# Cross-attention and mixture of experts: the order of the head on four engines is changed

## The reference

```python
q = layernorm(x) @ Wq.T ; k = v = ctx @ Wq.T
x = x + softmax(causal(q @ k.T / sqrt(128))) @ v
f = layernorm(x)
logits = f @ gate_W                       # 8 experts, the two largest are kept
cw = weights of the two largest, normalised, zero elsewhere
x = x + f + sum over e of cw[:, e] * (relu(f @ W1[e] + b1[e]) @ W2[e] + b2[e])
```

## Time and profile before

| | before |
|---|---|
| median of 3 runs | 132.61 us (131.99 to 133.05) |
| the profiled execution | 132.61 us, its span 130.8 us |
| TensorE busy (matmul) | 122.1 us, 93% |
| TensorE weight load busy | 92.1 us, 70% |
| VectorE busy | 106.1 us, 81% |
| ScalarE busy | 93.2 us, 71% |
| GpSimd busy | 53.1 us, 41% |
| TensorE's granted clock | full in all 40 slices |

### The profile page before, as it was taken

One profiled execution on the slowest core, in us unless ns is written; L12 is line 12 of the kernel. 1 busy time (PEld: TensorE's weight loads), 2 busy tenths in 40 slices (PEclk: granted clock), 3 DMA queues, 4 the chain that ended last, 5 costly groups with the idle time before them and its releaser, 6 DMA issues. The chain is left out here.

```text
span 130.8 us, 3269 instructions
## 1 busy us (share of the span) xinstructions
PE 122.1 (93%) x1165; PEld 92.1 (70%) x1165; DVE 106.1 (81%) x415; ACT 93.2 (71%) x189; POOL 53.1 (41%) x57
## 2 busy tenths in 40 slices
PE   6987798999989999999999999999999979999991
PEld 2674576777857769778877868778766757777690
DVE  0619998989999996968898996958998799867683
ACT  3247466999576955797679954994799558989830
POOL 7198156320084950321095840330277503345400
PEclk9999999999999999999999999999999999999999
DMA  3999900000000000200000000200000003000002
GB/s 95 319 286 295 291 28 8 0 0 0 5 0 0 0 8 0 80 0 5 0 0 5 0 3 0 80 5 0 0 3 8 0 0 85 3 0 0 5 0 80
DMA packets 9904, 5.54 MB, mean 42 GB/s; under 512 B 504, under 2 KB 9888, under 8 KB 9888
## 3 DMA queue, kind: packets, MB, share of 16 engines
q1 hardware_dynamic: 9744, 5.27, 14.7%
q10 hardware_dynamic: 144, 0.07, 0.2%
HBM read 4.28 MB, written 1.05 MB: 41 GB/s over the span
## 5 line engine op out<-in xcount | busy, mean ns | idle before, releaser
L658 POOL TENSOR_TENSOR h_lo<-h,h_hi 128x512 f16<-128x512 f32 x24 | 28.7, 1195 | 41.7 <-ACT h L543 41.3
L543 ACT ACTIVATE h<-psH,b1T 128x512 f32<-128x512 f32 x64 | 43.4, 690 | 1.1 <-PE psH L482 0.9
L542 ACT ACTIVATE h_hi<-psH,b1T 128x512 f16<-128x512 f32 x48 | 33.1, 689 | 14.9 <-PE psH L361 14.9
L832 DVE SCALAR_TENSOR_TENSOR acc<-psY,weight_y,acc 128x128 f32<-128x128 f32 x125 | 35.1, 341 | 3.2 <-PE psY L382 3.1
L357 PE MATMUL psH<-x_hi,w_hi 128*128 128x512 f16 x62 | 23.5, 379 | 1.0 <-ACT h L543 1.0
L816 DVE TENSOR_TENSOR h_lo<-h,h_hi 128x512 f16<-128x512 f32 x24 | 16.5, 688 | 8.8 <-ACT h L543 8.5
L361 PE MATMUL psH<-x_lo,w_hi 128*128 128x512 f16 x62 | 23.5, 379 | 0.0
L358 PE MATMUL psH<-x_hi,w_lo 128*128 128x512 f16 x62 | 23.5, 379 | 0.0
L382 PE MATMUL psY<-w_hi,h_hi 128*128 128x128 f16 x192 | 22.7, 219 | 0.0
L382 PE MATMUL psY<-w_lo,h_hi 128*128 128x128 f16 x192 | 22.7, 219 | 0.0
L382 PEld LDWEIGHTS psY<-w_hi,h_hi 128*128 128x128 f16 x192 | 15.4, 98 | 2.2
(11 more groups left out here) (175 smaller groups left out, 187.6 us busy)
## 6 DMA issues: line engine op xcount, KB each, us to landing
w_sb<-in_L_ffn_W_dram SPq DMA_DIRECT2D x8, 256.0 KB, 4.9
out_dram<-acc SPq DMA_DIRECT2D x3, 256.0 KB, 2.3
x_sb<-in_x_dram SPq DMA_DIRECT2D x2, 256.0 KB, 4.5
ctx_sb<-in_ctx_dram SPq DMA_DIRECT2D x2, 256.0 KB, 4.8
x_sb<-in_x_dram SPq DMA_DIRECT2D x1, 512.0 KB, 6.8
ctx_sb<-in_ctx_dram SPq DMA_DIRECT2D x1, 512.0 KB, 7.5
out_dram<-acc SPq DMA_DIRECT2D x2, 128.0 KB, 1.8
wq_sb<-in_L_xattn_Wq_dram ACTq DMA_DIRECT2D x1, 64.0 KB, 2.9
```

Of the source, the lines that this page charges most:

```text
L542: nc.scalar.activation(h_hi[:, C * (e % 2) + c, :], psH[c][:, :], ACT.Relu, bias=bias, scale=scale)
L543: nc.scalar.activation(h[:, C * (e % 2) + c, :], psH[c][:, :], ACT.Relu, bias=bias, scale=scale).then_inc(h_ready, 1)
L658: nc.gpsimd.tensor_tensor(h_lo[:, i, :], h[:, i, :], h_hi[:, i, :], ALU.subtract).then_inc(hlo0_ready, 1)
L832: last = nc.vector.scalar_tensor_tensor(out=o, in0=y, scalar=weight_y[:, g % 2, t, e:e + 1], in1=o, op0=ALU.mult, op1=ALU.add)
```

## The change

On SyncE's queue ctx of group 1 is loaded ahead of x. TensorE transposes ctx ahead of x, and takes `xf_transposes` of the second half behind group 1's scores. ScalarE copies ctx out ahead of x, and takes both `x_hi_part` ahead of `values_out`. VectorE takes the halves of group 0 one behind the other through residual, statistics, variance and norm, takes `x_lo_part` ahead of `mean_and_var` of group 1, and `w1_lo_part(1)` ahead of `mask_and_max(1)`. `small_parts` is cut in two: `gate_parts` stands ahead of `w1_lo_part(0)`, `b2_parts` behind `gate_choice(0)`; two semaphores join the gate parts, and `b2_product` waits for `small_lo`. The wait in `add_b2` is written as a formula with the value that it had.

```diff
             weights(0)
+            sp.dma_start(ctx_sb[:, TG:2 * TG, :], ctx_v[:, TG:2 * TG, :]).then_inc(ctx_in[1], 16)
             sp.dma_start(x_sb[:, TG:2 * TG, :], x_v[:, TG:2 * TG, :]).then_inc(x_in[1], 16)
-            sp.dma_start(ctx_sb[:, TG:2 * TG, :], ctx_v[:, TG:2 * TG, :]).then_inc(ctx_in[1], 16)
...
             def b2_product(g):
                 pe.wait_ge(catT_ready, g + 1)
+                pe.wait_ge(small_lo, 1)
...
+            pe.wait_ge(ctx_in[1], 16)
+            ctx_transposes(1, ALL, FIRST_BANKS)
             pe.wait_ge(x_in[1], 16)
             x_transposes(1, ALL, FIRST_BANKS)
-            pe.wait_ge(ctx_in[1], 16)
-            ctx_transposes(1, ALL, FIRST_BANKS)
             key_product(1, ALL, FIRST_BANKS)
             value_product(1, ALL, FIRST_BANKS)
-            for ts, banks in HALVES:
-                xf_transposes(0, ts, banks)
+            (first_half, first_banks), (second_half, second_banks) = HALVES
+            xf_transposes(0, first_half, first_banks)
             score_product(1, ALL, FIRST_BANKS)
+            xf_transposes(0, second_half, second_banks)
...
-            pe.wait_ge(small_lo, 1)
+            pe.wait_ge(gate_lo_ready, 1)
             logit_product(0)
...
+            ctx_out(1, ALL, FIRST_BANKS)
             x_out(1, ALL, FIRST_BANKS)
-            ctx_out(1, ALL, FIRST_BANKS)
             keys_out(1, ALL, FIRST_BANKS)
+            for ts, banks in HALVES:
+                x_hi_part(0, ts, banks)
             values_out(1, ALL, FIRST_BANKS)
-            for ts, banks in HALVES:
-                x_hi_part(0, ts, banks)
...
-            def small_parts():
+            def gate_parts():
                 dve.wait_ge(small_in, 16 * 5)
+                nc.vector.tensor_scalar(gate_hi[:, :], gate_sb[:, :], SW, None, ALU.mult).then_inc(gate_hi_ready, 1)
+                dve.wait_ge(gate_hi_ready, 1)
+                nc.vector.scalar_tensor_tensor(out=gate_lo[:, :], in0=gate_sb[:, :], scalar=SW, in1=gate_hi[:, :],
+                                               op0=ALU.mult, op1=ALU.subtract).then_inc(gate_lo_ready, 1)
+
+            def b2_parts():
                 dve.wait_ge(const_ready, 4)
...
+            gate_parts()
             w1_lo_part(0)
-            small_parts()
+            (first_half, first_banks), (second_half, second_banks) = HALVES
             for ts, banks in HALVES:
                 invert_sums(0, ts, chain)
             chain.wait()
-            for ts, banks in HALVES:
-                residual(0, ts, banks)
-            for ts, banks in HALVES:
-                chain.mark(second_stats(0, ts))
+            residual(0, first_half, first_banks)
+            chain.mark(second_stats(0, first_half))
+            residual(0, second_half, second_banks)
             chain.wait()
-            for ts, banks in HALVES:
-                second_variance(0, ts, chain)
+            second_variance(0, first_half, chain)
+            chain.link(second_stats(0, second_half))
+            second_variance(0, second_half, chain)
+            second_norm(0, first_half)
             dve.wait_ge(x_in[1], 16)
-            for t in range(TG, 2 * TG):
+            for t in range(TG, TG + 2):
+                row_stats(t)
+            second_norm(0, second_half)
+            for t in range(TG + 2, 2 * TG):
                 last = row_stats(t)
             chain.mark(last)
-            for ts, banks in HALVES:
-                second_norm(0, ts)
+            x_lo_part(0, first_half, first_banks)
+            x_lo_part(0, second_half, second_banks)
             chain.wait()
             mean_and_var(TG, 2 * TG, chain)
             w2_lo_part(0)
-            for ts, banks in HALVES:
-                x_lo_part(0, ts, banks)
+            w1_lo_part(1)
             mask_and_max(1, ALL, FIRST_BANKS)
-            w1_lo_part(1)
             gate_top(0, chain)
             gate_choice(0, chain, [lambda: w2_lo_part(1), lambda: hidden_lo(0, 0), None, None])
+            b2_parts()
             gate_weights(0, chain)
```

More of the change, by code:

```diff
@@ L183, in xattn_moe @@
         b1_ready, small_hi, small_lo = sem("b1_ready"), sem("small_hi"), sem("small_lo")
+        gate_hi_ready, gate_lo_ready = sem("gate_hi_ready"), sem("gate_lo_ready")
         w1hi_ready, w1lo_ready = [sem(f"w1hi_ready{p}") for p in range(PAIRS)], sem("w1lo_ready")
@@ L598, in _ @@
             copy(b1T[:, 1, :], psY[0][:, 0:E * C], b1_ready, scale=SH)
+            ctx_out(1, ALL, FIRST_BANKS)
             x_out(1, ALL, FIRST_BANKS)
-            ctx_out(1, ALL, FIRST_BANKS)
             keys_out(1, ALL, FIRST_BANKS)
-            values_out(1, ALL, FIRST_BANKS)
             for ts, banks in HALVES:
                 x_hi_part(0, ts, banks)
+            values_out(1, ALL, FIRST_BANKS)
             act.wait_ge(b1_ready, 1)
@@ L840, in add_b2 @@
                 dve.wait_ge(b2_ps, g + 1)
-                dve.wait_ge(y_used, Y_FREE + g * E + 3)
+                dve.wait_ge(y_used, Y_FREE + g * E + (B2_ADD + 1) // 2)
                 o = acc[:, bass.ts(g, TG), :]
@@ L913, in w2_lo_part @@
                                                op0=ALU.mult, op1=ALU.subtract).then_inc(w2lo_ready, 1)
-            def small_parts():
+            def gate_parts():
                 dve.wait_ge(small_in, 16 * 5)
+                nc.vector.tensor_scalar(gate_hi[:, :], gate_sb[:, :], SW, None, ALU.mult).then_inc(gate_hi_ready, 1)
[3 more added lines that the diff above has]
+            def b2_parts():
                 dve.wait_ge(const_ready, 4)
-                nc.vector.tensor_scalar(gate_hi[:, :], gate_sb[:, :], SW, None, ALU.mult)
                 rows = [slice(32 * q, 32 * q + E) for q in range(3)]
@@ L923, in small_parts @@
                 dve.wait_ge(small_hi, 1)
-                nc.vector.scalar_tensor_tensor(out=gate_lo[:, :], in0=gate_sb[:, :], scalar=SW, in1=gate_hi[:, :],
-                                               op0=ALU.mult, op1=ALU.subtract)
                 nc.vector.scalar_tensor_tensor(out=b2_cat[rows[2], :], in0=b2_rows[rows[2], :], scalar=SW,
```

## The result

The changed kernel is slower by 1.2%: the ratio to the kernel before is 1.0124, with a 95% interval from 1.0066 to 1.0181 (about 134.2 us against 132.6), and 1.0121 (1.0076 to 1.0167) when it was timed again. The forecast had the direction and the mechanism of its first half, but 1.15 us where 1.6 us are lost. In about a third of its executions TensorE's clock falls to half for some 3 us (see e5): these take about 136.2 us, are left out of the ratios, and put the plain median at 135.2, above the forecast's range of 132.4 to 134.3.

The account below looks back on a forecast made before the run. ScalarE's unbroken run from the gate's first result was taken to set the pace; a gate 0.4 us late and b2's held split, partly absorbed, gave 132.61 + 1.15 = 133.75 us, range 132.4 to 134.3.

Parts of the forecast that it names:

- what bounds: Head into loop: ScalarE's unbroken run sets the pace, and it waits for the gate's first result on VectorE, `below`.
- the first relu: ScalarE at the end of the head: starts at about 20.6, 0.65 us ahead of 21.28.
- the relu leads: Rival: ScalarE's run not bound by `below`, so the first relu's 0.65 us reach the loop; 131.95 us, chance 0.10.
- The keys: TensorE in the head: the keys start at 15.10 instead of 15.60, since ScalarE copies ctx first.
- `x_hi` of the second half: ScalarE in the head: starts at 18.62 against 18.95, 0.33 us earlier, as transposes behind the scores eat 0.89.
- group 1's variance behind `x_lo`: VectorE in the head, taken to decide the case: power and masks come later, `below` at 23.34 against 22.95.
- b2 held: VectorE behind the gate's choice: b2's multiplications wait until GpSimd's `h_lo` ends, 1.33 to 1.67 us later; chance 0.45.
- a short second multiplication: Within b2's split, held: the long one of the three is short this time, making the delay 1.33 instead of 1.67.
- The bound from `b2` under `w_hi`: Rival, b2 not held: 0.66 us later behind the choice, 133.0 us; chance 0.32, shared with a short power.
- The row against being held: Evidence in the head: b2's three multiplications ran to 13.00 while GpSimd's `w_hi` ran from 12.08 to 13.57.
- "Later by 1.33 to 1.67, it moves TensorE by 1.27 to 1.61": Expert 1's `h_lo` on VectorE delays its second product on TensorE; after absorption, +0.95 to +1.29 us, middle 1.15.
- "the head slips": Rival at the head's start: `gate_parts` waits for loads or GpSimd, up to 0.6 us lost; about 134.3 us, chance 0.13.

Follow-up runs that it names:

- e5: The changed kernel with eight more matmuls of zeros on TensorE where it waits for expert 1's `h_lo`; ratio to the kernel before 1.0145.
- e1: The changed kernel with b2's split left out (its matmuls still run); ratio to the kernel before 1.0009.
- e7: The changed kernel with the second half's xf transposes again ahead of group 1's scores; ratio to the kernel before 1.0066.
- e2: The changed kernel with group 1's `mean_and_var` ahead of both `x_lo`; ratio to the kernel before 1.0115.
- e8: The changed kernel with group 1's variance ahead of `x_lo`, `w1_lo_part(1)` behind the masks, b2's multiplications on ScalarE, its subtraction behind expert 0's sum; ratio to the kernel before 0.9962.
- e9: The kernel before with b2's multiplications on ScalarE, its subtraction on VectorE behind expert 0's sum, and `gate_parts` where `small_parts` stood; ratio 0.9936.
- e3: The changed kernel with GpSimd's `h_lo` of expert 2 made to wait for VectorE's `h_lo` of expert 1; ratio to the kernel before 1.0082.
- e4: The kernel before with only `gate_parts` where `small_parts` stood and `b2_parts` behind `gate_choice(0)`; ratio 1.0039.
- e10: e9 with `w1_lo_part(1)` ahead of group 1's masks; ratio to the kernel before 0.9929, 131.7 us.

## Why the prediction was right or wrong

**Right: what bounds.** ScalarE's unbroken run starts with `below`, not with the first relu. In the kernel after the relu is 0.96 us earlier (10.57 from the first mask against 11.53; 0.65 was forecast), and ScalarE then waits 1.96 us for `below` (1.7 was forecast) and the loop starts later. The rival "the relu leads" is out, by this wait and by e1.

**Right, with sizes.** The keys 0.49 us earlier (0.5 forecast); `x_hi` of the second half 0.42 (0.33); group 1's variance behind `x_lo`, and through it `below` 0.37 later (0.39). e7 shows that the transposes behind the scores feed this term and e1 that it is worth 0.36 us on the end. That `mean_and_var` behind `x_lo` decides it was not shown as I meant to show it: e2 freed the variance and ran into the hold of `w1_lo`. e8, where the variance is first and the masks too, has `below` 1.04 us earlier than the kernel after; it changes the two places together.

**Right: b2 held.** The three multiplications end 0.53 us after GpSimd's `h_lo` (27.07 and 26.54), and `chosen` ends 1.40 us later than before. The forecast was 1.67, or 1.33 with a short second multiplication, and the short case is the one that came. The bound from `b2` under `w_hi` (0.66) is out. The row that stood for it was misread. One by one, the long multiplication before and the first one after:

```profile
12.21 0.56 DVE L921 TENSOR_SCALAR b_cat<-b_rows 8x128 f16<-8x128 f32 x1
```

```profile
25.55 1.06 DVE L929 TENSOR_SCALAR b_cat<-b_rows 8x128 f16<-8x128 f32 x1
```

The other two after it take 0.22 us each, so 0.22 is the length of one that nothing holds. The 0.56 before began 0.13 us behind GpSimd's `w_hi` (12.08) and was held too, by the first half microsecond of it. The row against being held was thus a shorter hold, and the 0.86 us for the three had that hold in it. GpSimd and VectorE of e9 show the same on `w1_lo` of pair 0, which takes 0.68 alone:

```profile
11.60 1.50 POOL L683 TENSOR_SCALAR w_hi<-w_sb 128x512 f16<-128x512 f32 x1
```

```profile
11.61 1.16 DVE L914 SCALAR_TENSOR_TENSOR w_lo<-w_sb,w_hi 128x512 f16<-128x512 f32 x1
```

The Trainium skill (SBUF — State Buffer, Who interferes with whom) says that whichever of the two comes second is blocked for the whole instruction of the other. Under `h_lo` the trace agrees (1.06 us); under `w_hi` it shows a hold in a part of the 1.50 us only, and the rows decide.

**Wrong: "Later by 1.33 to 1.67, it moves TensorE by 1.27 to 1.61".** This is the step that failed. It moved expert 1's `h_lo` later with its old length of 0.69 us. Its start is as forecast, 1.40 late. But at that place GpSimd's `h_lo` of expert 2 begins, 0.04 us ahead of it, and it takes 1.66. TensorE's second part of expert 1 is 2.25 us late instead of 1.3 to 1.6, group 1's second variance 1.91 (36.09 before, 38.33 after) instead of 0.95 to 1.29, the end 1.87, and the time 1.6 instead of 1.15. The row of GpSimd's next `h_lo` was not among those that this step uses, though the paragraphs before it price just such a meeting; with it the sum would have been 1.15 + 0.97, less some 0.2 to 0.5, or 134.2 to 134.5, an estimate from these rows and from what was given back in e3. e3 shows the cause: the same start, no overlap, 0.69 us.

**Not foreseen: the clock.** With a wait of 1.7 us on TensorE its clock halves in a third of the executions, for about 2 us of time each. The sum had no term for this, and it is what puts the plain median (135.2) above the range. It follows from the same failed step: by the forecast the wait would have been 0.7 us, and at 0.7 us (e3) it didn't happen in 12.

**The rival "the head slips"** did not happen: `gate_parts` delayed nothing that TensorE waited for. "I give them no gain" for the earlier residual holds only in that nothing was left over: the first xf transposes start 7.19 us from the first mask after (17.27), and before they had waited for the norm until 8.00 (17.75), so without it the gain of the keys would not have come through. And e4 shows that in the kernel before the same 1.1 us were worth 0.75.

## What to carry to other kernels

When an instruction is moved on VectorE, look up what GpSimd runs at the new time, for the moved instruction and for each that it pushes: a hold by one GpSimd instruction (here 0.84 us on b2's first multiplication, 0.97 on `h_lo`, and 1.09 in e2) is as much as the work moved, or more. Which one starts first decides: put the two-tensor instruction that others wait for 0.3 us ahead of the GpSimd one, and the hold falls on the other. And before a gain at one engine's first task is counted, look at the start of the unbroken run that sets the pace: what it waits for last is the only thing that is worth bringing forward.

## What the runs showed of the hardware

- VectorE instructions with two tensors in SBUF were held nearly to the end of a GpSimd TENSOR_TENSOR of 128x512 that had begun first: `h_lo` 1.66 us for 0.69 (after), `w1_lo` 1.77 for 0.68 (e2), the gate's 128x32 product 1.03 for 0.19. 0.04 us ahead were enough (after). The other way round GpSimd's is longer: `base_sum` 1.57 for 1.28 (e10).
- The 8x128 TENSOR_SCALAR was held in the same way: 1.06 us for 0.22 (after, e4).
- GpSimd's one-input TENSOR_SCALAR `w_hi` (1.50 us) held a two-tensor VectorE instruction only in its first half microsecond: `w1_lo` of pair 0 took 1.16 us where it began 0.01 behind `w_hi` (e9), and 0.68 where it began 0.76 behind it (12.22 against 11.46 in the first trace of the kernel after). A TENSOR_SCALAR was held there too (0.56 for 0.22, before), and again near the end of `w_hi`: `gate_hi` 0.44 for 0.17, begun 1.08 into it (e9).
- The masks, with one tensor in SBUF and one in PSUM, were not held under `base_sum` (0.34 us in e10).
- GpSimd's power on four columns did not hold VectorE: `w1_lo`, begun 0.36 us into it, took 0.68 (after). The power took 1.31 us where a two-tensor VectorE instruction was running as it began (before, after, e10), and 1.01 where the next one began 0.55 us into it (e2).
- TensorE's clock fell to half near 30.8 us after TensorE had been idle since 29.3, and in 12 of 39 executions of kernels with such a wait; in none of 70 in which the wait there was 0.7 us or less.
